# Working the last chunk and the last filter group in halves, and loading spectra one chunk ahead, in a fused attention, MLP and Fourier-filter kernel

## The reference

```python
# block 1: attention with 12 heads and relative positions, then an MLP
x   = x + attention(layernorm(x)) @ proj_w + proj_b
x   = x + gelu(layernorm(x) @ w1 + b1) @ w2 + b2            # 192 -> 768 -> 192
# block 2: a Fourier filter, then an MLP
h   = layernorm(x) * g1 + be1
xf  = rfft2(h, axes=(height, width))                        # 48 x 25 frequencies
o1  = relu(cmul(xf, w1) + b1)                               # 8 blocks of 24 channels, complex
o2  = softshrink(cmul(o1, w2) + b2, 0.01)
x   = irfft2(o2) + h + x
out = x + gelu(layernorm(x) @ fc1_w + fc1_b) @ fc2_w + fc2_b
```

## Time and profile before

| | |
|---|---|
| median of 3 runs | 1050.36 us (1047.97 to 1052.39) |
| the profiled execution | 1051.88 us, of which its span from first to last instruction is 1050.10 us |
| TensorE busy, granted clock | 1002.8 us of the span, mean 0.969 of 2.4 GHz |
| VectorE, ScalarE, GpSimd busy | 849.3, 700.5, 337.4 us |
| first MLP stage, its end | about 799 to 899 us of the span |
| filter stage | about 899 to 952 us |
| second MLP stage | about 952 to 1050 us |

### The profile page before, as it was taken

The page is one execution under the profiler, slowest core; times in us unless marked ns, Lnnn a source line. Parts: engine busy times, 40 slices in busy tenths (PEclk is TensorE's granted clock), DMA queues, the critical chain, the costliest instruction groups (busy, mean ns, idle before and its releaser), DMA issues.

```text
span 1050.1 us, 36800 instructions
## 1 busy us (share of the span) xinstructions
PE 1002.8 (95%) x15948; PEld 707.7 (67%) x15948; DVE 849.3 (81%) x1741; ACT 700.5 (67%) x1004; POOL 337.4 (32%) x161
## 2 busy tenths in 40 slices
PE   5978999999999999999999999999989999998998
PEld 3556267776776767777777777777647776664666
DVE  5869999999999999999999999999716576133664
ACT  4767177777787777777787777877884454141555
POOL 4440242332435352423434242424214554100111
PEclk9985599999999999999999999999999999999999
DMA  4787754442513231313131322212100010322231
GB/s 123 203 222 212 225 148 131 130 109 60 118 54 97 58 96 49 99 48 99 40 97 52 85 63 69 79 49 76 42 23 12 24 47 13 81 59 75 81 92 57
DMA packets 75158, 91.80 MB, mean 87 GB/s; under 512 B 15341, under 2 KB 67378, under 8 KB 74805
## 3 DMA queue, kind: packets, MB, share of 16 engines
q1 hardware_dynamic: 74967, 89.45, 31.5%
q10 hardware_dynamic: 30, 0.02, 0.0%
HBM read 65.63 MB, written 23.21 MB: 85 GB/s over the span
## 4 chain that ended last, share of the span: by engine, by line
PE 78%; DVE 11%; DMA 4%; ACT 4%; issue 2%; POOL 1%; SPq 0%; DVEq 0%; ACTq 0%
PE ps L1165 40%; PE ps L1325 19%; PE ps L1160 14%; DVE mx_p L1632 2%; DVE stage_lo L1601 2%; PE ps L1178 1%; ACT hid_f L1093 1%; DVE stats L94 1%; POOL rstd L120 1%; DVE xh L112 1%; PE ps L1271 1%; PE ps L1490 1%; PE ps L1513 1%; ACT hid L1087 1%; DMA u_sb<-u_d 1%
## 5 line engine op out<-in xcount | busy, mean ns | idle before, releaser
L1632 DVE TENSOR_REDUCE mx_p<-ps 128x1 f32<-128x464 f32 (+1 forms) x1080 | 607.2, 629 | 16.9 <-PE ps L1165 6.0
L1040 ACT ACTIVATE prob<-ps 128x768 f32<-128x768 f32 x648 | 495.2, 810 | 166.3 <-PE ps L1165 165.8
L1165 PE MATMUL ps<-kc,qc 112*32 112x464 f16 (+1 forms) x4320 | 456.8, 369 | 3.0 <-DVE stage_lo L1601 2.9
L1165 PE MATMUL ps<-qv,ka 113*32 113x384 f16 x5184 | 400.2, 327 | 3.4 <-ACT prob L1040 2.3
L837 POOL COPY qv<-qv 48x6144 f16<-48x6144 f16 x36 | 190.8, 5299 | 354.6 <-DMA qv<-kq_d 354.2
L1325 PE MATMUL ps<-prob,v_ext 128*32 128x384 f32 x2592 | 289.3, 485 | 0.5 <-ACT prob L1040 0.5
L1165 PEld LDWEIGHTS ps<-qv,ka 113*32 113x32 f16 x5184 | 214.3, 97 | 76.8 <-issue 18.5
L1165 PEld LDWEIGHTS ps<-kc,qc 112*32 112x32 f16 x4320 | 172.7, 95 | 100.2 <-DVE mx_p L1632 28.2
L1325 PEld LDWEIGHTS ps<-prob,v_ext 128*32 128x32 f32 x2592 | 116.9, 110 | 12.1 <-ACT prob L1040 1.2
L1160 PE MATMUL ps<-xnt_all,w_up 96*128 96x384 f16 x432 | 75.0, 326 | 2.8 <-ACT hid_f L1093 2.8
L120 POOL TENSOR_TENSOR rstd<-rstd 96x4 f32<-96x4 f32 x24 | 26.9, 1122 | 150.7 <-DVE rstd L102 150.0
(11 more groups left out here) (107 smaller groups left out, 820.1 us busy)
## 6 DMA issues: line engine op xcount, KB each, us to landing
qv<-rel_d SPq DMA_DIRECT2D x216, 144.0 KB
qc<-rel_d SPq DMA_DIRECT2D x22, 216.0 KB, 4.1
xin<-in_x SPq DMA_DIRECT2D x12, 288.0 KB, 3.5
kq_d<-khl SPq DMA_DIRECT2D x24, 144.0 KB, 2.3
q_h<-kq_d SPq DMA_DIRECT2D x9, 288.0 KB, 4.6
q_w<-qw_d SPq DMA_DIRECT2D x9, 288.0 KB, 6.5
rel_d<-stage_hi SPq DMA_DIRECT2D x4, 648.0 KB, 7.4
rel_d<-stage_lo SPq DMA_DIRECT2D x4, 648.0 KB, 8.8
```

The costliest lines, as they stand in the source:

```text
L1040: nc.scalar.activation(prob[:, s4(p, s), :].rearrange("p (a b) -> p a b", a=2), ps[:, 3 + 2 * (s % 2):5 + 2 * (s % 2), 0:CW], ACT.Exp).the ...
L1165: ins = nc.tensor.matmul(ps[c:c + 32, bank, 0:w], l[:, c:c + 32], r, start=True, stop=True, tile_position=(0, c))
L1632: nc.vector.tensor_reduce(mx_p[:, q * GT + k // MP, k % MP:k % MP + 1], ps[:, slot, 0:min(MW, N - k % MP * MW)], AX, ALU.max).then_inc(uni ...
```

## The change

It has three parts. The last chunk's chain from `down` to the stored spectrum is cut into tiles 0 and 2 (half 0) and tiles 1 and 3 (half 1). For that chunk `down` puts tiles 1 and 3 into banks 4 and 5 and announces each half by itself; DVE runs a new `last_norm`, half 0 from sum to `h1` and then half 1; POOL takes the power per half; PE transforms each half with one matmul of 384 columns once its `h1` is there, with 12 unneeded matmuls between the halves and 44 behind them, instead of 34 before and 44 behind; ACT copies each half into `u_last`, which lies in the memory of `f_x`, and SP stores each. In the filter's last group, `layer2` announces its two PSUM banks one by one; DVE's three instructions, `inverse`, and ACT's copy go half by half, and of 14 unneeded matmuls 4 are left. In the second MLP stage SP issues `load_u2(1)` right behind `load_u2(0)`, ahead of `to_wide_tiles(0)`, and `block1(c)` loads chunk c + 2 where it loaded c + 1. Buffer `u_sb` stays single: the load of c waits until `inverse_w(c - 1)` has read it, as before.

```diff
+        u_last = f_x[:, :, :].rearrange("p a b -> p (a b)")[0:4 * KF, 0:CT * C].rearrange("p (t c) -> p t c", c=C)
...
-            store_u1(NC - 1)
-            sp.wait_ge(u_out, 16 * NC)
+            for a in range(2):
+                sp.wait_ge(u_ok, NC + a)
+                sp.dma_start(u1_t[:, (NC - 1) * CT + a:NC * CT:2, :], u_last[:, a:CT:2, :]).then_inc(u_out, 16)
+            sp.wait_ge(u_out, 16 * (NC + 1))
...
             def block1(c, more):
-                if more:
-                    load_u2(c + 1)
+                if c + 2 < NC:
+                    load_u2(c + 2)
...
             load_u2(0)
+            load_u2(1)
             to_wide_tiles(0)
...
-                norm_root(pool, nc, rstd, ln3, c)
+                if more:
+                    norm_root(pool, nc, rstd, ln3, c)
+                else:
+                    for a in range(2):
+                        pool.wait_ge(ln3["var"], NC + a)
+                        nc.gpsimd.tensor_tensor(rstd[:, 1, a:CT:2], rstd[:, 0, a:CT:2], rstd[:, 2, a:CT:2],
+                                                ALU.pow).then_inc(ln3["rstd"], 1)
...
-            spectrum(NC - 1)
+            for a in range(2):
+                act.wait_ge(fw_ps, NC + a)
+                nc.scalar.activation(u_last[:, a:CT:2, :],
+                                     ps[0:4 * KF, 6 + a, 0:2 * C].rearrange("p (b c) -> p b c", b=2),
+                                     ACT.Copy).then_inc(u_ok, 1)
...
                 for a in range(2):
+                    if g == G - 1:
+                        act.wait_ge(fi_ps, G + a)
                     ins = nc.scalar.activation(
...
+                apart = i == 0 and c == NC - 1
+
                 def down_tile(t):
-                    return ps[0:W, 2 + t // 2, (t % 2) * C:(t % 2 + 1) * C]
+                    return ps[0:W, (4 if apart and t in late else 2) + t // 2, (t % 2) * C:(t % 2 + 1) * C]
...
                 for t in (0, 2):
-                    lo_products(t)
+                    ins = lo_products(t)
+                if apart:
+                    ins.then_inc(sems["dn_ps"], 1)
...
             pe.wait_ge(u_ok, NC - 1)
-            stay_awake(34, 4, hid[:, 0, 0, :])
-            dft(NC - 1)
-            stay_awake(44, 4, hid[:, 0, 0, :])
+            for a in range(2):
+                pe.wait_ge(h1_ok, NC + a)
+                mm(ps[0:4 * KF, 6 + a, 0:2 * C].rearrange("p (b c) -> p b c", b=2), dft_w[:, :],
+                   h1[:, a:CT:2, :]).then_inc(fw_ps, 1)
+                stay_awake((12, 44)[a], 0, hid[:, 0, 0, :])
...
+                    if g == G - 1 and j == 1:
+                        ins.then_inc(f2_ps, 1)
                 ins.then_inc(f2_ps, 1)
...
                 for a in range(2):
+                    if g == G - 1:
+                        pe.wait_ge(fo_ok, G + a)
                     ins = mm(ps[0:2 * S, 6 + a, 0:FN], dft_hi[:, :], f_o[:, a, :])
+                    if g == G - 1 and a == 0:
+                        ins.then_inc(fi_ps, 1)
...
-            stay_awake(14, 3, hid[:, 0, 0, :])
+            stay_awake(4, 3, hid[:, 0, 0, :])
             inverse(G - 1)
...
+            def last_norm():
+
+                x1_c = x1[:, (NC - 1) * CT:NC * CT, :]
+                dve.wait_ge(x1b_ok, NC)
+                dve.wait_ge(r3_ok, NC - 1)
+                for a in range(2):
+                    dve.wait_ge(up0["dn_ps"], NC + a)
+                    nc.vector.scalar_tensor_tensor(out=y_sb[:, a:CT:2, :], in0=ps[0:T, 2 + 2 * a:4 + 2 * a, a * C:(a + 1) * C],
+                                                   scalar=1 / WS, in1=x1_c[:, a:CT:2, :],
+                                                   op0=ALU.mult, op1=ALU.add).then_inc(up0["sum"], 1)
...
+                    for t in (a, a + 2):
+                        ins = nc.vector.bn_stats(stats[:, t, :], y_sb[:, t, :])
...
+                    dve.wait_ge(ln3["rstd"], NC + a)
+                    dve.wait_ge(fw_ps, NC - 1)
+                    for t in (a, a + 2):
+                        ins = nc.vector.scalar_tensor_tensor(out=h1[:, t, :], in0=xh2[1][:, t, :],
+                                                             scalar=rstd[:, 1, t:t + 1], in1=rows[0:T, 2, :],
+                                                             op0=ALU.mult, op1=ALU.add)
+                    ins.then_inc(h1_ok, 1)
...
-            for g in range(G):
-                dve.wait_ge(f2_ps, g + 1)
+            def shrink(count, g, h):
+
+                dve.wait_ge(f2_ps, count)
...
+            for g in range(G - 1):
+                shrink(g + 1, g, slice(0, 2))
+            for a in range(2):
+                shrink(G + a, G - 1, slice(a, a + 1))
```

More of the change, by code:

```diff
@@ L918, in block0 @@
                     skip(c - 1)
-                norm_root(pool, nc, rstd, ln3, c)
+                if more:
[5 more added lines that the diff above has]
+                                                ALU.pow).then_inc(ln3["rstd"], 1)
             def skip(c):
-                pool.wait_ge(h1_ok, c + 1)
+                pool.wait_ge(h1_ok, c + 1 if c + 1 < NC else NC + 1)
                 nc.gpsimd.tensor_tensor(r3[:, ds(c * CT, CT), :], h1[:, :, :], y_sb[:, :, :],
@@ L1521, in inverse @@
                 for a in range(2):
+                    if g == G - 1:
+                        pe.wait_ge(fo_ok, G + a)
                     ins = mm(ps[0:2 * S, 6 + a, 0:FN], dft_hi[:, :], f_o[:, a, :])
+                    if g == G - 1 and a == 0:
+                        ins.then_inc(fi_ps, 1)
                 ins.then_inc(fi_ps, 1)
             pe.wait_ge(fw_neg, 1)
-            pe.wait_ge(up0["sum"], NC)
-            pe.wait_ge(u_ok, NC)
+            pe.wait_ge(up0["sum"], NC + 1)
+            pe.wait_ge(u_ok, NC + 1)
             pe.wait_ge(f_pads, 1)
@@ L1688, in lo_of_hidden @@
                                             ALU.subtract).then_inc(sems["lo"], 1)
+            def last_norm():
[7 more added lines that the diff above has]
+                                                   op0=ALU.mult, op1=ALU.add).then_inc(up0["sum"], 1)
+                    dve.wait_ge(up0["sum"], NC + a)
+                    dve.nop(nofuse=True)
+                    for t in (a, a + 2):
+                        ins = nc.vector.bn_stats(stats[:, t, :], y_sb[:, t, :])
+                    ins.then_inc(ln3["stats"], 1)
+                    dve.wait_ge(ln3["stats"], NC + a)
+                    dve.nop(nofuse=True)
+                    for t in (a, a + 2):
+                        ins = nc.vector.bn_aggr(mv[:, t, :], stats[:, t, :])
+                    ins.then_inc(ln3["mean"], 1)
+                    dve.wait_ge(ln3["mean"], NC + a)
+                    nc.vector.tensor_scalar(rstd[:, 0, a:CT:2], mv[:, a:CT:2, 1], EPS, None,
+                                            ALU.add).then_inc(ln3["var"], 1)
+                    for t in (a, a + 2):
+                        ins = nc.vector.scalar_tensor_tensor(out=xh2[1][:, t, :], in0=y_sb[:, t, :],
+                                                             scalar=mv[:, t, 0:1], in1=rows[0:T, 1, :],
+                                                             op0=ALU.subtract, op1=ALU.mult)
+                    ins.then_inc(h1_mul, 1)
+                    dve.wait_ge(h1_mul, NC + a)
+                    dve.wait_ge(ln3["rstd"], NC + a)
+                    dve.wait_ge(fw_ps, NC - 1)
+                    for t in (a, a + 2):
+                        ins = nc.vector.scalar_tensor_tensor(out=h1[:, t, :], in0=xh2[1][:, t, :],
+                                                             scalar=rstd[:, 1, t:t + 1], in1=rows[0:T, 2, :],
+                                                             op0=ALU.mult, op1=ALU.add)
+                    ins.then_inc(h1_ok, 1)
             def block0(c, more):
@@ L1696, in block0 @@
                     lo_of_hidden(c, up0, tiles)
+                    last_norm()
+                    return
                 mlp_sum(c, up0, x1b_ok, lambda: wait_used(dve, r3_ok, c))
@@ L1714, in _ @@
             chunks(block0)
-            for g in range(G):
-                dve.wait_ge(f2_ps, g + 1)
+            def shrink(count, g, h):
+                dve.wait_ge(f2_ps, count)
                 dve.wait_ge(f_b2_ok, 1)
-                nc.vector.tensor_tensor(f_y[:, :, :], ps[0:FP, 4:6, 0:FN],
-                                        f_b2[:, :, :, :].rearrange("p (a g) f c -> p a (g f c)", a=2),
+                nc.vector.tensor_tensor(f_y[:, h, :], ps[0:FP, 4:6, 0:FN][:, h, :],
+                                        f_b2[:, :, :, :].rearrange("p (a g) f c -> p a (g f c)", a=2)[:, h, :],
                                         ALU.add).then_inc(fy_ok, 1)
-                dve.wait_ge(fy_ok, g + 1)
-                nc.vector.tensor_scalar(f_c[:, :, :], f_y[:, :, :], -LAM, LAM, ALU.max, ALU.min).then_inc(fc_ok, 1)
-                dve.wait_ge(fc_ok, g + 1)
+                dve.wait_ge(fy_ok, count)
```

(8 more changed lines are left out.)

## The result

The changed kernel took 1043.26 us, median of five executions (1042.86 to 1045.19), against 1050.36 us (1047.97 to 1052.39) for the kernel before, which is now a median of five too, with the same value as that of the three known before. The recorded ratio, which is not simply the quotient of the two medians, is 0.9929 with a 95% interval of 0.991 to 0.9948, so 5.5 to 9.5 us less. The forecast was 1044.5 us, 5.9 less, with a range of 1041.8 to 1048.0.

The account below looks back on a forecast made before the run. TensorE bounds the filter's middle; at three edges between stages, chains through other engines and transfers bound it. Gains of 2.8, 1.8 and 1.3 us sum to 5.9, taking 1050.36 to 1044.5 us, range 1041.8 to 1048.0.

Parts of the forecast that it names:

- the chain of half 1: Last chunk of the first MLP: the chain from `y_sb` to `h1` takes 4.02 us per half, against 5.62 whole.
- the power on POOL: Last chunk: 1.12 us, counted as unchanged by halving because nearly all fixed; bounds nothing saved and 0.56 us.
- the two paths behind: Ahead of `transform(0)`: copy, store and load (903.75 us) and the 44 unneeded matmuls (904.15) end level; start about 904.2.
- The 150 KB store: Store of the last half's spectrum ahead of the filter: 2.7 us expected, bounds 2.4 and 3.23.
- The Trainium skill's point against small vector tiles: Vector instructions pay fixed latency each, 0.15 us here, lengthening the chains of half 1 and the filter's last group.
- The first copy: Filter's last group, ACT: after group 3's store lands by 948.3 us, it is over at 948.9, ahead of the second.
- (A): Rival: the clock falls once at the thinned edge into the filter, losing nearly 1.7 us; 1046.2 us, chance 0.13.
- (B): Rival: the last chunk's halves do not overlap as laid out, gaining 1 us instead of 2.8; 1046.3 us, chance 0.08.
- (D): Rival: the early spectrum load wins nothing, because `up(0)` is set by something else; 1045.8 us, chance 0.06.
- (C): Rival: the clock falls at the edge and stays down into the filter; two groups would give 1058 us; chance 0.03.

Follow-up runs that it names:

- `dft(4)` early: Changed kernel with `dft(4)` on PE ahead of tiles 1 and 3 of the last `down`, not behind them; 1042.8 us, ratio 0.9927.
- 34 behind: Changed kernel with 34 instead of 44 unneeded matmuls behind the last half; 1045.26 us, ratio 0.9947.
- part 1 alone: Kernel before with only the last chunk of the first MLP in halves; 1044.97 us, ratio 0.9946.
- part 3 alone: Kernel before with only the spectra loaded one chunk ahead in the second MLP; 1048.45 us, ratio 0.9971.
- without fill: Changed kernel without the 12 and the 44 unneeded matmuls at the last chunk; 1045.89 us, ratio 0.995.
- 14 left: Changed kernel with 14 unneeded matmuls, not 4, between the last `layer2` and the inverse; 1042.54 us in one execution.
- early and 38: Changed kernel with `dft(4)` ahead of tiles 1 and 3 of the last `down` and 38 unneeded matmuls instead of 44; 1042.59 us, ratio 0.9909.

## Why the prediction held

**Part 1, forecast 2.8, measured 3.2.** Half 0 started 1.94 us behind S (forecast 1.89), and its `h1` 5.60 behind S (5.49), held by `dft(4)` as laid out, which the run with `dft(4)` early showed. Half 1 started 6.26 behind S, as forecast (6.24). The term that was too dear is the chain of half 1: 4.02 forecast, 893.92 - 890.41 = 3.51 measured. Of the 0.51 less, the power on POOL makes 0.33: it took 0.79 us for two values, where I had counted the whole 1.12 and called it nearly all fixed. Aggregation makes 0.14, with 0.24 instead of 0.38. Against that the lone half's matmul took 0.89 us and not 0.73: the pair's 1.46 us is 0.89 and 0.57, not twice 0.73.

That the two paths behind are level was wrong. The 150 KB store landed in 2.17 us (34 behind, its chain above), below my lower bound of 2.4, so the load is there 6.3 us behind the end of the last half's matmul, while the 44 matmuls end at 7.1. The gain came out near the forecast because the start of the transform is the later of the two, and the matmuls, the later one, were priced right (7.15). That the store was priced too dear cost the forecast nothing. The Trainium skill's point against small vector tiles (fixed cost per instruction) held in kind: the middle step of bias and softshrink, which reads and writes SBUF alone, takes 0.67 us for 960 elements and 0.42 for 480. It did not decide anything.

**Part 2, forecast 1.8, measured 1.7.** ACT's second copy ended 6.36 us behind the start of `layer2` (forecast 6.29). The first copy has less slack than I said: it waited for the store of group 3 and started 4.88 us behind `layer2`'s start, where I had that store landed at 4.29, and it was over 0.34 us before the second half's data came. The timeline shows the wait:

```profile
943.88 0.57 ACT L1143 ACTIVATE f_u<-ps 96x480 f32<-96x480 f32 x1 [3.75 <-DMA u_d<-f_u]
...
944.79 0.57 ACT L1143 ACTIVATE f_u<-ps 96x480 f32<-96x480 f32 x1 [0.34 <-PE ps L1176]
```

**Part 3, forecast 1.3, measured 1.55, above its upper bound of 1.45.** Of the 0.25 us between them in the first pair of profiles, 0.17 is that a matmul starts before the modelled end of the one ahead (959.63 + 1.47 against 960.93), and 0.07 that `up(0)` followed 1.30 and not 1.37 us behind. The larger fault is of kind: I read PE's wait of 1.31 us as a size of the code, and it is one draw; the same code waited 0.64 to 2.49. The mechanism, PE's wait gone and nothing lost later, held.

**The rivals.** (A) did not happen at that edge: in all seven executions with part 1 and its matmuls between the halves, A is as its own chain makes it, and the granted clock is 1.00 from 886 to 906 us. But the fall at 815 us, on which I built (A), taught the main thing of this study: it is there in five of twelve executions, with the last chunk's code of before (two of four) and with that of the change (three of eight). Between the first two profiles it is 1.66 of the 1.81 us ahead of S: the same transposes at 815.91 and 815.75, the next width transform at 821.24 and 819.42. (B) fell with part 1 alone, (D) with part 3 alone. (C) did not occur; without fill the clock did stay down into the filter, and it cost 3.6 us there, but not the 14 of two whole groups: before 910 us it was back at 1.00.

So the parts are worth 3.3 + 1.7 + 1.55 = 6.5 us by the means of the stretches, against 5.9 forecast. What the medians show beyond that, 0.6 us, is inside the interval; the untouched code's scatter (S 882.35 to 888.61) is more than any part. That the time came within 1.2 us of the forecast is in part luck: the median of the kernel before alone was 1050.36, 1051.94, 1050.98 and 1052.28 in the four series.

## What to carry to other kernels

Cut both traces at instructions that they share and compare stretches: the gains of parts 1 and 2 (3.3 and 1.7 us) could be told here to a few tenths from one or two profiles, while whole times with 5 to 10 executions left overlapping intervals. When a chain's last link is made shorter, count the fill beside it anew: 44 matmuls that were hidden before became the limit. A wait for a transfer in one profile is one draw; if the change takes the transfer off the path, its gain is a spread, not a number, and the spread goes too: C was 10.20 to 10.22 in the eight executions with part 3.

## What was not expected of the hardware

The clock's fall near 815 us is not decided by the instructions and idle times around it: with the same ones (idle 1.03 to 1.05 and 0.95 to 0.96 us, 1.19 us of matmuls between) it fell in five executions and held in seven. What does decide it stays open. The kernel before, profiled twice, fell both times, and the changed kernel neither time, so the traces of this fall alone don't prove chance. The times without a trace speak for it: of the twenty executions of the kernel before that ran beside the three parts, ten had a mean granted clock of 0.971 and took 1049.2 to 1051.6 us, and ten had 0.968 or 0.969 and took 1052.3 to 1053.7.

Nor is it the only place. Summed over windows of 10 us ahead of S, the clock below full speed cost from about 27.3 us (14 left) to 34.1 (part 1 alone, 34 behind, early and 38), with the others near 29.0, 30.7 and 32.4: steps of 1.7 us, the price of one fall. Near 780 us, for instance, it fell in part 1 alone and in early and 38, and in none of the others. With this cost taken off, the spread of S shrinks from 6.3 to 4.0 us; the rest of it is not explained.

The Trainium skill, "TensorE: Matmul & The Clock Gate", Part 1, says of the rise to full clock under steady matmuls that its point varies from run to run. The rows here are of a fall, which varies as well.

One window of each kind near 815 us, first part 1 alone, then the changed kernel:

```profile
815.00:820.00 5.00, 4.74 (x37) 4.74 (x38) 1.16 (x2) 2.07 (x3) 3.60 (x2) 0.66 0.00 0
```

```profile
815.00:820.00 5.00, 4.25 (x46) 4.02 (x47) 1.91 (x4) 2.07 (x3) 3.59 (x2) 1.00 0.00 0
```

The first store of x3 (288 KB) took 2.52 to 4.33 us in the four executions with the same code around it; what lengthened it stays open.
